# Second pass of a quantized feed-forward: the first clip of five images in six goes from VectorE to GpSimd, and VectorE casts the middle tile of every image

## The reference, cut to what matters

```
def _quantize_activations_groupwise(x):      # 5 groups of 6 images, the last 2 images give zero
    gamma = jnp.max(jnp.abs(ag))
    xq = clip(ag * 128 / (gamma + EPS), -128 + EPS, 128 - EPS)
def _bitlinear(x, W, b):
    y = jnp.einsum('btc,oc->bto', x, sign-like(W)) + b
    return _quantize_activations_groupwise(y)
h   = gelu(_bitlinear(x, W1, b1))            # 96 -> 384
out = _bitlinear(h, W2, b2)                  # 384 -> 96
t   = t + out
```

## Time and profile before

| | |
|---|---|
| median of 3 runs | 782.65 us (781.4 to 784.79) |
| the profiled execution's own time | 783.51 us |
| its span, first to last instruction | 781.8 us |
| mean granted TensorE clock | 0.978 |
| busy share PE, DVE, ACT, POOL | 94%, 86%, 64%, 26% |

### The profile page before, as it was taken

One profiled execution on the slowest core, in us unless ns is written; L12 is line 12 of the kernel. 1 busy time (PEld: TensorE's weight loads), 2 busy tenths in 40 slices (PEclk: granted clock), 3 DMA queues, 4 the chain that ended last, 5 costly groups with the idle time before them and its releaser, 6 DMA issues.

```text
span 781.8 us, 15334 instructions
## 1 busy us (share of the span) xinstructions
PE 732.1 (94%) x4806; PEld 483.1 (62%) x4806; DVE 672.8 (86%) x2006; ACT 498.5 (64%) x701; POOL 203.9 (26%) x240
## 2 busy tenths in 40 slices
PE   5799779999999999999999999999999999999991
PEld 3465457666667666677666676666677555555550
DVE  2577488999899999899999899999899678999997
ACT  1544455566666566566566666666665699999980
POOL 2352122232322232322233322323321000211210
PEclk8889999999999999999999999999999999999996
DMA  9880101111111111111111111111110001574446
GB/s 209 187 200 1 32 16 47 32 32 46 32 31 45 32 31 46 31 31 46 31 31 46 31 31 46 31 37 40 31 31 15 25 8 16 76 139 62 62 62 139
DMA packets 17773, 41.40 MB, mean 53 GB/s; under 512 B 4663, under 2 KB 4949, under 8 KB 17749
## 3 DMA queue, kind: packets, MB, share of 16 engines
q1 hardware_dynamic: 14552, 33.27, 16.5%
q0 software_dynamic: 2688, 7.23, 6.7%
q10 hardware_dynamic: 509, 0.60, 0.3%
HBM read 22.28 MB, written 18.67 MB: 52 GB/s over the span
## 4 chain that ended last, share of the span: by engine, by line
PE 63%; DVE 16%; ACT 7%; issue 6%; SPq 3%; DMA 2%; POOL 2%; DVEq 1%; ACTq 0%; POOLq 0%
PE slot L1057 15%; PE slot L1041 11%; PE slot L1268 6%; PE slot L1244 6%; PE slot L904 5%; PE slot L1063 5%; PE slot L1068 5%; DVE stage L1574 4%; PE slot L1106 4%; ACT stage L785 4%; SPq L464 3%; DVE stage L1561 2%; DVE y2max L1678 2%; PE slot L1306 1%; PE slot L1302 1%
## 5 line engine op out<-in xcount | busy, mean ns | idle before, releaser
L1057 PE MATMUL slot<-hT,w2s 128*96 128x392 f32 x384 | 136.8, 492 | 2.2 <-ACT hT L778 2.2
L1528 DVE TENSOR_SCALAR tok<-tok,ln_mv,ln_rs 112x96 f32<-112x96 f32 x434 | 109.2, 322 | 7.0 <-POOL ln_rs L610 4.4
L778 ACT ACTIVATE hT<-slot,b1c,w_unit 128x784 f32<-128x784 f32 x96 | 96.0, 1004 | 20.2 <-PE slot L1041 20.2
L610 POOL TENSOR_TENSOR ln_rs<-ln_ve,pow_half 112x7 f32<-112x7 f32 x62 | 91.9, 1482 | 4.8
L1057 PEld LDWEIGHTS slot<-hT,w2s 128*96 128x96 f32 x384 | 60.4, 163 | 48.5 <-issue 43.8
L1068 PE MATMUL slot<-big,W1b 96*128 (+1 forms) x360 | 89.2, 329 | 0.0
L1063 PE MATMUL slot<-big,W1b 99*128 (+1 forms) x360 | 84.6, 329 | 0.0
L840 ACT ACTIVATE hT<-slot,s 128x784 f32<-128x784 f32 x90 | 80.2, 914 | 5.5 <-DVE stage L1561 3.2
L1534 DVE TENSOR_REDUCE ymax<-slot 128x784 f32 (+1 forms) x90 | 83.4, 955 | 0.0
L607 POOL TENSOR_TENSOR ln_ve<-ln_mv,ln_eps 112x7 f32<-112x7 f32 x62 | 12.6, 203 | 270.3 <-DVE ln_mv L1522 267.4
L580 POOL TENSOR_TENSOR xn_lo<-xn,xn_hi 96x784 f16<-96x784 f32 x32 | 53.8, 1681 | 109.6 <-DVE tok L1528 109.6
(11 more groups left out here) (228 smaller groups left out, 1458.3 us busy)
## 6 DMA issues: line engine op xcount, KB each, us to landing
xs<-in_x SPq DMA_DIRECT2D x32, 294.0 KB, 2.9
out<-t2T SPq DMA_DIRECT2D x32, 294.0 KB, 2.6
big<-in_x SPq DMA_DIRECT2D x7, 1176.0 KB, 16.7
out<-t2T POOLq DMA_DIRECT2D x24, 294.0 KB, 4.3
big<-out SPq DMA_DIRECT2D x1, 1764.0 KB, 10.5
out<-big SPq DMA_DIRECT2D x6, 294.0 KB, 2.7
big<-in_x SPq DMA_DIRECT2D x2, 588.0 KB, 24.6
con<-shape_consts ACTq DMA_DIRECT2D x1, 445.5 KB, 6.6
```

The costliest lines, as they stand in the source:

```text
L610: nc.gpsimd.tensor_tensor(ln_rs[n][:, :], ln_ve[n][:, :], pow_half[0:TOK, 0:CHUNKS], ALU.pow).then_inc(ln_rstd[n], 1)
L778: nc.scalar.activation(hT[:, t, :].rearrange("p (a n) -> p a n", a=2), halves(t, P), ACT.Relu, scale=w1_unit[:, t:t + 1], bias=b1c[:, t:t ...
L1057: ins = mm(S[k][0:C, h, 0:HALF], w2s[:, v, t, :], hT[:, t, h * HALF:(h + 1) * HALF], start=t == 0, stop=t == TILES - 1, skip_group_check=True)
L1528: ins = V.tensor_scalar(dst[:, j, :], src[:, j, :], ln_mv[n][:, j, 0:1], ln_rs[n][:, j:j + 1], ALU.subtract, ALU.mult)
```

## The change

GpSimd's loop over the 24 images that are finished in the loop makes, ahead of the DMA of image b, the first clip of image b + 1, unless b + 1 is the first of its group. VectorE keeps the first clip of the first image of each group (four times), and for the other 20 only waits on the same counting semaphore `qv_ready`. ScalarE no longer casts tile 1; VectorE casts it in all 30 images instead of in 15.

```diff
-            with pool.Fori(0, FINISHED) as m:
-                for r in range(2):
-                    b = 2 * m + r
-                    pool.wait_ge(o_ready, b + 1)
-                    pool.dma_start(out_bcn[b], t2T[r][:, :], accum_op=ALU.add).then_inc(o_stored[r], 16)
+            def clip_next(b):
+                nc.gpsimd.tensor_scalar(qv[b % 2][:, :], y2_all[:, b, :], s2[:, b // QB:b // QB + 1], Q_CLIP,
+                                        ALU.mult, ALU.min).then_inc(qv_ready, 1)
+
+            for b in range(QIMAGES - QB):
+                if b % QB == 0:
+                    pool.wait_ge(qv_ready, b + 1)
+                if (b + 1) % QB > 0:
+                    clip_next(b + 1)
+                pool.wait_ge(o_ready, b + 1)
+                pool.dma_start(out_bcn[b], t2T[b % 2][:, :], accum_op=ALU.add).then_inc(o_stored[b % 2], 16)
...
-                gelu_hi(0, 1, 0)
...
-                    if r == 0:
-                        gelu_hi(b, 1, r)
                     y2_out(b - 1)
...
-                if r == 1 and t == SPLIT - 1:
+                if t == SPLIT - 1:
                     dve.wait_ge(gelu_ready, 3 * b + t + 1)
                     V.tensor_copy(h_hi[r][:, t, :], gel[:, t, :]).then_inc(hi_cast, 1)
-                    dve.wait_ge(hi_cast, m + 1)
+                    dve.wait_ge(hi_cast, b + 1)
                 else:
-                    dve.wait_ge(hi_parts, 3 * m + 2 * r + t + 1)
+                    dve.wait_ge(hi_parts, b + 1)
...
-            def clipped(g, m, r):
+            def clipped(g, m, r, whole=False):
                 b = 2 * m + r
-                dve.wait_ge(s2_ready, g + 1)
-                V.tensor_scalar(qv[r][:, :], y2_all[:, b, :], s2[:, bass.ds(g, 1)], Q_CLIP,
-                                ALU.mult, ALU.min).then_inc(qv_ready, 1)
+                if whole:
+                    dve.wait_ge(s2_ready, g + 1)
+                    V.tensor_scalar(qv[r][:, :], y2_all[:, b, :], s2[:, bass.ds(g, 1)], Q_CLIP,
+                                    ALU.mult, ALU.min).then_inc(qv_ready, 1)
                 dve.wait_ge(qv_ready, b + 1)
...
-                        clipped(g - 1, m - QB // 2, 0)
+                        clipped(g - 1, m - QB // 2, 0, scale)
```

## The result

The kernel after takes 801.6 us, the median of 4 runs (800.03 to 802.89). The kernel before took 783.12 beside it (4 runs). The ratio is 1.0236, with a 95% interval of 1.0211 to 1.0261: the change makes the kernel slower by 2.4%. The forecast was 813, its own range 787 to 822. The sign and the place were right, and the size was 1.7 times too large: +30.5 against +18.5. In the profiled executions the difference is 800.03 - 783.51 = 16.5 us.

What follows compares the result with a forecast made beforehand. VectorE was taken to set the pace, 29.08 us a group, only 0.8 above TensorE. 27.15 + 5 x 1.94 = 36.9 a group, +31 over four groups, -0.5 at the tail: 814.0 profiled, forecast 813, range 787 to 822.

Steps and rivals of the forecast that it cites:

- TensorE's floor and VectorE's load: Second pass, finishing groups of six images: TensorE alone needs 28.3 us a group, VectorE 27.15 after the change without collisions.
- the term used: VectorE's added casts, second pass: 0.59 us each, three more a group (+1.77); no cost in the 624 to 658 stretch.
- VectorE gets one hold of 2.38 us: Finishing groups: GpSimd's clip and VectorE block each other at the SBUF, 2.38 us in each of five images a group.
- the loss per clip: VectorE in finishing groups: 1.50 us if the maximum hides its part, 2.38 if nothing is hidden; half taken, 1.94.
- the tail: End of the kernel: the last first clip (0.61 us) leaves VectorE and the scale chain uses most of it, -0.5 us.
- GpSimd's price: GpSimd's new 96 x 784 clip in the second pass: 2.58 us, at 3.05 ns an element, lower end 1.68.
- Rival 1: VectorE in finishing groups: operations pass GpSimd's clip at no cost, the change wins 3.5 us, 779 us; chance 0.25.
- Rival 2: Finishing groups: weak collision at a clip's start only, 0.2 to 0.5 us a clip, 782 us; chance 0.10.
- Rival 3: Finishing groups: full collision and TensorE's clock falls once a group, +4 us, 817, up to 826; chance 0.07.
- The dependencies: GpSimd's clips in finishing groups come on time, needing 3.4 of 4.85 us an image; DMAs late only at a group's first image.

Runs made afterwards that it cites:

- e3: Kernel after the change, with GpSimd's clip cut to 96 x 8 elements and the rest of it left out for 20 images: 779.48 us, ratio 0.9961.
- e1: Half of the change on the kernel before: VectorE casts the middle tile of every image and keeps all first clips: 788.96 us, ratio 1.0071.
- e4: Kernel before, plus the same 20 GpSimd clips written to a buffer nobody reads: 800.3 us, ratio 1.0231.
- e7: The probe: kernel before with a measuring stretch ahead, VectorE chains alone, then beside a GpSimd operation; one-input chain 3.09 us alone, 4.24 beside a clip.
- e2: Other half of the change on the kernel before: GpSimd makes 20 first clips, ScalarE keeps its casts: 801.89 us, ratio 1.024.

## Why the prediction was right, and where its size was off

**TensorE's floor and VectorE's load: right.** I took 28.3 and 27.15 us a group. With the clip's work gone (e3) a group takes 28.11, with TensorE busy throughout and VectorE for 26.93. The casts cost 6.2 us where they stand alone (e1), against 7.1 by the term used, and nothing in the 624 to 658 stretch.

**"VectorE gets one hold of 2.38 us": right in kind, wrong in form.** The term of the sum that was mis-sized is the loss per clip: 1.94 us in the prediction, 1.13 measured in the kernel after and 0.78 in e4. I had made it of a clip of 2.58 us that keeps VectorE out from beginning to end, less half a maximum. The clip is longer than that, 2.90 us alone, but it keeps VectorE out in two bursts, together 1.15 us in the probe. The full hold was read from a GpSimd operation with two inputs, and beside such a one the probe has it too (1.63 us). Carrying it over to an operation with one input made the size too large. With 1.13 in place of 1.94 the prediction's own sum gives 27.15 + 5.65 = 32.8 us a group (32.7 measured) and +3.7 x 4 = +14.9; with the tail 783.5 + 14.9 - 0.5 = 797.9, against the 800.0 of the profiled execution. That 1.13 is so near the 1.15 of the small one-input operations is partly chance: 14.7 of the 22.6 us are lost by two-input rests, and such a chain loses 0.65 in the probe. In the kernel after, the single stops are longer (1.17 and 1.10 us in the image shown) than in the probe, and other images have none beside a clip's start. GpSimd's DMA issue lies close to them there (1.11 us instead of 0.8 to 0.85). Which part of a stop it has was not tried.

The Trainium skill, SBUF — State Buffer, "Who interferes with whom", has the pair locked for the whole instruction. Beside the two-input GpSimd operation the trace agrees (1.63 us lost, 1.68 long). Beside the clip it does not: by that rule the small operations of e7 would have come to rest for 2.9 us, and the sum would be the 813 of the forecast. The measurement decides: 1.15 us in two bursts. Its exemption of the reduction agrees (3.59 us with and without the clip).

**GpSimd's price: right in order, low by a tenth.** From two small rows I took 3.05 ns an element, so 2.58 us; alone it takes 2.90. In the kernel it takes 3.5 us, since the collision holds it up as well, which I had named without a number.

**Rival 1, no collision (0.25): wrong.** Its evidence was a two-input operation that was not slowed 0.47 us into a GpSimd operation of 0.78. By the probe, two-input operations are stopped once beside a clip and run at their pace for the rest of it. The row would be such a free part, and could not speak for one-input operations. **Rival 2 (0.10)** had the nearer mechanism, "only the reading at a clip's start holds the port", but not the second burst. By its bounds, 0.2 to 0.5 us, it is out: 1.13 was measured.

**Rival 3, the clock falls too (0.07): in part.** In the kernel after the clock falls at 668.6 us, where TensorE had waited 2.89 us for a rest, and that group is 34.40 - 32.69 = 1.7 us longer than the next. It falls again at about 778 us, in the last image: its last matmul groups take 1.54 and 2.38 us, where before they took 0.86 and 1.48 (+1.6). I had one per group and +4. Together these 3.3 us more than make up the 2.1 that the sum above lacks. In e2 they do come once a group.

**The dependencies: right.** VectorE shows no wait for a GpSimd clip in the kernel after.

## What to carry to other kernels

Work moved to an idle engine is free only if the two engines can read and write at the same time: before moving, look in the trace for a pair of instructions of these two engines side by side, and see whether either is longer than its twin alone. The pair has to be of the kinds that will meet: here a GpSimd operation with two inputs cost VectorE 1.63 us, and a longer one with one input 0.65 to 1.15. What such an operation costs depends on what lies beside it, so its place in the order matters as well as its length: here the whole change cost 18.5 us with the clips where they fell, and 10 when they started beside a reduction. And compare the relieved engine with the next one first: here only 3.3 us were to be had (e3), however cheap the clip.

## What was not expected of the hardware

Beside chains of small VectorE operations, a GpSimd tensor_scalar of 96 x 784 float32 (2.90 us) stops VectorE in two bursts of about 0.6 us, at its start and its end, and not in between. Two-input VectorE operations lose only the first (+0.65), one-input ones both (+1.15), reductions neither. Beside full-size two-input operations the one stop has the same size (+0.64) but comes later. A GpSimd tensor_tensor of the same shape stops a two-input VectorE operation for 1.63 us, about its whole length. GpSimd is held up as well: the same clip takes 2.89 to 5.53 us by what lies beside it. In the kernel single stops reached 1.17 us; why they are longer there than in the probe is open.
